# The last group's FFN in sixteen blocks of 256 tokens, with the layer norm of its first half among the blocks of the second

## The chip, the cores and the metric

The kernel runs on one NeuronCore of a Trainium2 chip. The time is the device time of one execution in microseconds (us). The kernel before takes 508.56 us (median of three runs, 507.5 to 508.71). Five engines work side by side and wait for one another through semaphores: PE (TensorE, the matmuls), DVE (VectorE), ACT (ScalarE), POOL (GpSimd) and SP (SyncE, which issues every DMA here).

## The reference

The input is 64 sequences of 64 tokens of 256 numbers, with a 64-number condition for each sequence. Layer 0 is a transformer block whose norms are scaled and shifted by the condition; layer 1 is a layer norm with a conditioned bias. What matters here is the end of it, cut to its core:

```
x   = x + a_alpha * attention(ada_rmsnorm(x))
y   = ada_rmsnorm(x)                                  # gamma, beta from the condition
ffn = silu(y @ gate_w.T) * (y @ hidden_w.T) @ out_w.T + out_b   # 256 -> 1024 -> 256
x   = x + f_alpha * ffn
out = (x - mean) * rsqrt(var + 1e-5) * weight + bias
out = (out + tanh(cond @ lin_w.T + lin_b)) * weight + bias
```

All is in float32. The matmuls with weights are made of three products of split operands: high part with high, low with high, high with low.

## The kernel before, in words

The 4096 tokens are cut into 8 groups (`g`) of 512 tokens, that is 8 sequences, or 4 tiles of 128 tokens. Each engine has its program written out by hand, in the order in which its instructions stand; nothing is reordered. The attention of group `g` is laid among the FFN blocks of group `g - 1`. `last(g)` is the program of each engine for the last group: first its attention among the FFN blocks of group 6 (there called `f`), and then the FFN of group 7 alone, with the layer norm of group 6 among its blocks, and at the end the layer norm of group 7 with nothing beside it. The change touches this last part only.

The 1024 hidden units are cut into 8 chunks of 128 (`CH = 8`). A block is one chunk for all 512 tokens and goes through the engines like this:

- PE, `gate_hidden` (L645): 12 matmuls with 512 columns, six into a gate bank and six into a hidden bank. The moving operand is `x2s`, in a high and a low part; ACT makes the high part (L893) and POOL the low (`x2_split`, L1379). For block 0 the program sorts the twelve, so that the four which need the low part come last.
- ACT, `tanh` (L867), reads the gate bank.
- DVE, `feed`: L1185 makes (tanh + 1) * gate, L1189 multiplies by half the hidden bank. Both leave their result in `act_t`.
- ACT, `hidden_hi` (L874): the rounded copy of `act_t`, the high part of `hs`.
- POOL, `hidden_lo` (L1413): the difference of the two, the low part of `hs`.
- PE, `ffn_out` (L662): 12 matmuls with 256 columns, which add the block to the output of 4 tiles in banks 0 and 1.

ACT takes `tanh(c)`, `hidden_hi(c)`, `tanh(c + 1)`, and so on, in this order, and `hidden_hi(c)` waits for DVE's second step of block c. In the last group `gate_hidden` alternates between two pairs of banks (2 and 3, 4 and 5), `act_t` and `hs` have two slots each, and `ffn_out(c - 2)` stands behind `gate_hidden(c)`: a lag of two blocks.

Behind the last `ffn_out`, DVE does `residual2` (L1201, L1204: times f_alpha, plus the residual `x2c`, on 4 tiles at once), the layer norm's sums (`sums_x3`, L1068, one instruction for each tile), means and variances (`stats_x3`, L1073 to L1077), the reciprocal root (`rsqrt`, L1022 to L1031: one estimate and three Newton rounds, ten small instructions, each of which waits for the one before), `mean_x3` (L1081), and then `finish_last` (L1212, L1217), two instructions for each of tiles 0 to 2. Tile 3 goes through ACT (`scale_x3`, L899) and POOL (L1497, L1499). SP stores the four tiles with a DMA for each (L412). For group 6 the same norm stands on DVE behind block 3 of group 7, on ACT (L899) behind block 4, and on POOL (L1403, L1409) behind block 4.

## Time and profile before

| | |
|---|---|
| median of 3 runs | 508.56 us (507.5 to 508.71) |
| the profiled execution's own time | 508.42 us |
| its span | 506.6 us |
| mean granted clock of PE | 0.987 of full speed |
| PE busy | 478.7 us, 94% of the span |
| DVE busy | 393.4 us, 78% |
| POOL busy | 271.4 us, 54% |
| ACT busy | 241.4 us, 48% |
| DMA | 44.21 MB, mean 87 GB/s |

The span is from the first to the last thing that the profiler saw; the execution's own time is 1.82 us longer. Starts are counted from the span's start. PE is busy throughout except for the last stretch. A share of busy time doesn't tell which engine decides: that is read from the waits at one place.

### The profile page before, as it was taken

The page shows a single profiled execution, that of the slowest core. Times are in us where ns is not written, and L with a number is a line of the kernel's source. Part 1 is how long each engine was busy: PE and PEld are TensorE (multiplying, and loading weights), DVE is VectorE, ACT ScalarE, POOL GpSimd, SP SyncE. Part 2 cuts the span into 40 slices and gives each one's busy share as a digit, 9 for nine tenths or more (in the row PEclk, how much of TensorE's full clock was granted, in tenths as well). Part 3 has the DMA queues.
Part 4 walks back from the last instruction along what each step waited for, and adds up shares of the span by engine and source line. Part 5 has one row for each costly group of instructions (what it writes and reads, how often), then busy time and mean ns, then how long its engine had stood idle before and what let it go on. Part 6 is the DMA issues. An engine that isn't in the chain of part 4 may idle for free.

```text
span 506.6 us, 11675 instructions
## 1 busy us (share of the span) xinstructions
PE 478.7 (94%) x4456; PEld 400.6 (79%) x4456; DVE 393.4 (78%) x776; ACT 241.4 (48%) x348; POOL 271.4 (54%) x179
## 2 busy tenths in 40 slices
PE   7888989999999999999999999999999999999990
PEld 4666878897878978888888978798788978888890
DVE  5868679778886888878895888878897789685636
ACT  3774743338352653438362563537354484414240
POOL 3447456454269445783269445684259543716471
PEclk9989999999999999999999999999999999999996
DMA  8463370206413082214503073023703062400131
GB/s 190 148 190 118 91 203 12 56 2 165 128 23 85 9 224 58 63 41 126 164 18 86 0 210 80 24 80 85 203 2 103 1 161 48 112 15 8 34 65 61
DMA packets 36058, 44.21 MB, mean 87 GB/s; under 512 B 3136, under 2 KB 31040, under 8 KB 36032
## 3 DMA queue, kind: packets, MB, share of 16 engines
q1 hardware_dynamic: 36032, 43.85, 32.5%
q8 instruction: 18, 0.29, 0.2%
q14 instruction: 8, 0.07, 0.1%
HBM read 35.18 MB, written 4.47 MB: 78 GB/s over the span
## 4 chain that ended last, share of the span: by engine, by line
PE 72%; DVE 7%; DMA 5%; ACT 4%; POOL 4%; issue 4%; SPq 2%; ACTq 0%; DVEq 0%; POOLq 0%
PE banks L645 26%; PE banks L662 16%; PE banks L465 7%; PE banks L563 5%; PE banks L497 4%; PE banks L595 4%; DMA row_b<-rows_dram 3%; PE banks L581 3%; PE banks L586 3%; DVE qpar L1113 1%; PE banks L423 1%; POOL hs L1413 1%; DMA xtok<-x_in 1%; DVE act_t L1185 1%; SPq L312 1%
## 5 line engine op out<-in xcount | busy, mean ns | idle before, releaser
L645 PE MATMUL banks<-x2s,gh 128*128 128x512 f32 x768 | 191.5, 398 | 5.1 <-DVE act_t L1185 4.6
L645 PEld LDWEIGHTS banks<-x2s,gh 128*128 128x128 f32 x768 | 139.9, 188 | 37.7 <-DVE act_t L1185 6.0
L1413 POOL TENSOR_TENSOR hs<-act_t,hs 128x512 fp32r<-128x512 f32 x64 | 83.0, 1301 | 96.0 <-ACT hs L874 96.0
L662 PE MATMUL banks<-wout,hs 128*128 128x256 f32 x768 | 105.1, 286 | 2.2 <-POOL hs L1413 2.1
L662 PEld LDWEIGHTS banks<-wout,hs 128*128 128x128 f32 x768 | 97.8, 188 | 8.1 <-POOL hs L1413 3.1
L874 ACT ACTIVATE hs<-act_t 128x512 fp32r<-128x512 f32 x64 | 40.3, 630 | 92.1 <-DVE act_t L1189 86.1
L867 ACT ACTIVATE act_t<-banks 128x512 f32<-128x512 f32 x64 | 38.2, 597 | 74.9 <-PE banks L645 71.9
L1185 DVE SCALAR_TENSOR_TENSOR act_t<-act_t,banks 128x512 f32<-128x512 f32 x64 | 43.9, 686 | 38.5 <-ACT act_t L867 37.3
L1136 DVE RECIPROCAL work_c<-banks 128x512 f32<-128x512 f32 x16 | 53.7, 3354 | 5.1 <-PE banks L581 5.1
L465 PE MATMUL banks<-xs,wqk 128*128 128x512 f32 x192 | 47.1, 393 | 2.3 <-POOL xs L1365 1.6
L1189 DVE SCALAR_TENSOR_TENSOR act_t<-act_t,banks 128x512 f32<-128x512 f32 x64 | 44.0, 687 | 5.9 <-PE banks L645 1.7
L465 PEld LDWEIGHTS banks<-xs,wqk 128*128 128x128 f32 x192 | 34.9, 188 | 10.1 <-POOL xs L1365 2.0
L1119 DVE TENSOR_REDUCE smax<-banks 128x16 bf16<-128x1024 f32 x32 | 37.6, 1217 | 2.7 <-PE banks L526 2.7
L1374 POOL TENSOR_TENSOR x2g<-x2g,tabs 128x512 f32<-128x512 f32 x16 | 16.4, 1043 | 42.6 <-DVE x2g L1178 42.6
L1389 POOL TENSOR_TENSOR x2c<-x,row_b 128x1024 f32<-128x1024 f32 x8 | 19.1, 2390 | 34.0 <-DMA row_b<-rows_dram 29.9
L563 PE MATMUL banks<-qpair,kpar 64*128 64x128 f32 x512 | 36.5, 282 | 0.8 <-issue 0.4
L563 PEld LDWEIGHTS banks<-qpair,kpar 64*128 64x128 f32 x512 | 31.2, 187 | 4.1 <-issue 2.7
L882 ACT ACTIVATE pt<-banks 128x1024 f32<-128x1024 f32 x32 | 31.9, 1018 | 4.2 <-PE banks L568 2.0
L822 ACT ACTIVATE kpair<-banks,cst 128x1024 bf16<-128x1024 f32 x16 | 17.0, 1110 | 22.4 <-PE banks L465 22.4
L1153 DVE TENSOR_TENSOR banks<-banks,row_aa 128x512 f32<-128x512 f32 x16 | 11.1, 694 | 19.4 <-PE banks L595 19.4
L1369 POOL TENSOR_TENSOR os<-work_c,os 128x512 fp32r<-128x512 f32 x16 | 20.6, 1289 | 8.1 <-ACT os L888 8.1
L497 PEld LDWEIGHTS banks<-wv,xs 128*128 128x128 f32 x192 | 24.1, 191 | 0.6
(118 smaller groups left out, 687.5 us busy)
## 6 DMA issues: line engine op xcount, KB each, us to landing
xtok<-x_in SPq DMA_DIRECT2D x8, 512.0 KB, 5.5
work_c<-xn SPq DMA_DIRECT2D x16, 256.0 KB, 3.5
xres<-x_in SPq DMA_DIRECT2D x8, 512.0 KB, 7.1
row_aa<-rows_dram SPq DMA_DIRECT2D x16, 256.0 KB, 6.7
row_af<-rows_dram SPq DMA_DIRECT2D x16, 256.0 KB, 5.9
row_b<-rows_dram SPq DMA_DIRECT2D x16, 256.0 KB, 6.4
shift<-rows_dram SPq DMA_DIRECT2D x16, 256.0 KB, 6.1
y<-final SPq DMA_DIRECT2D x7, 512.0 KB, 3.2
```

The lines of the kernel that those rows point to most:

```text
L465: last = mm(banks[:, base + m, :], wqk[:, a, k, c:c + P], xs[:, b, k, :], start=(n == 0), stop=(n == 5))
L497: last = mm(banks[:, base + t // 2, D * (t % 2):D * (t % 2) + D], xs[:, a, k, P * t:P * t + P], wv[:, b, k, :], start=(n == 0), stop=(n == 5))
L563: mm(region(i, half), kpar[r, h, b], qpair[r, h, :, L * b:L * b + L], start=(i == 0), stop=False)
L645: last = mm(banks[:, base + part, :], gh[:, a, k, w:w + P], x2s[:, b, k, :], start=(n == 0), stop=(n == 5))
L662: last = mm(banks[:, t // 2, D * (t % 2):D * (t % 2) + D], hs[:, c % 2, b, P * t:P * t + P], wout[:, a, c, :], start=(c == 0 and a == b an ...
L867: nc.scalar.activation(act_t[:, c % 2, :], banks[:, base, :], ACT.Tanh, scale=0.5)\
L874: nc.scalar.activation(hs[:, c % 2, 0, :], act_t[:, c % 2, :], ACT.Copy).then_inc(h_hi, 1)
L1119: V.tensor_reduce(smax[:, :, 8 * n:8 * n + 8], banks[:, base:base + 2, :].rearrange("p a (x c) -> p a x c", c=L), AX.X, ALU.max).then_inc( ...
L1136: V.reciprocal(work_c[:, 0, :], banks[:, den_bank, :]).then_inc(o_steps, 1)
L1185: V.scalar_tensor_tensor(out=a, in0=a, scalar=1.0, in1=banks[:, base, :], op0=ALU.add, op1=ALU.mult).then_inc(h_steps, 1)
L1189: V.scalar_tensor_tensor(out=a, in0=a, scalar=0.5, in1=banks[:, base + 1, :], op0=ALU.mult, op1=ALU.mult).then_inc(h_steps, 1)
L1413: tt(hs[:, c % 2, 1, :], act_t[:, c % 2, :], hs[:, c % 2, 0, :].bitcast(F32), ALU.subtract)\
```

## The change

The FFN of group 7 is done in two halves of 256 tokens, eight blocks for tiles 0 and 1 and then eight for tiles 2 and 3, so 16 half blocks `n`. A half block has 12 matmuls of 256 columns in `gate_hidden_half`, 6 in `ffn_out_half`, and instructions of half the width on ACT, DVE and POOL. There are three pairs of banks (6 and 7, 2 and 3, 4 and 5) instead of two and four half slots of `act_t` and `hs` instead of two whole ones, and `ffn_out_half(n - 3)` stands behind `gate_hidden_half(n)`. The first half's output lies in bank 0, the second's in bank 1. The order of the matmuls of block 0 is no longer sorted.

The norm of group 6 is spread on DVE behind half blocks 3, 4 and 5, on ACT behind 6 and 7, and on POOL behind 7 to 10, in halves. `residual2` of the first half of group 7 stands on DVE behind half block 11, its sums and variances behind 12, its reciprocal root behind 13; ACT scales tiles 0 and 1 (two instructions) between half blocks 14 and 15; POOL weights and shifts them behind its last `hidden_lo_half`. Behind the last half block, DVE does tiles 2 and 3 alone. There are three stores at the end: tiles 0 and 1 together, tile 2, tile 3. In the diff, lines inside `build` stand eight columns further left than in the file.

```diff
 WARM_LOADS, WARM_MAX, WARM_OUTPUT, WARM_NORM = 3, 4, 16, 4
-LAST_DVE = 3
+HALF = TOK // 2
+BLOCKS = 2 * CH
...
     return not isinstance(g, int) or g > 1
+def half_slot(a, n):
+    s = n % 4
+    return a[:, s // 2, ..., HALF * (s % 2):HALF * (s % 2) + HALF]
+def half_base(n):
+    return (6, 2, 4)[n % 3]
+def x3_half(h):
+    return banks[:, h, :].rearrange("p (t n) -> p t n", t=2)
...
     def load_shift(f):
         if later(f):
-            sp.wait_ge(final_steps, FS * f)
+            sp.wait_ge(final_steps, FS * f + (FS if is_last(f) else 0))
         load_rows(shift, R_SHIFT, f, ld_shift)
...
     load_af(GROUPS - 1)
-    store(GROUPS - 2)
+    sp.wait_ge(final_steps, FS * (GROUPS - 2) + 2 * FS)
+    sp.dma_start(out_v[GROUPS - 2], final[:, :, :]).then_inc(out_stored, 16)
     load_shift(GROUPS - 1)
-    for t in range(TT):
-        if t < LAST_DVE:
-            sp.wait_ge(last_dve, LAST_DVE + t + 1)
-        else:
-            sp.wait_ge(last_pool, 2 * (t - LAST_DVE) + 2)
+    sp.wait_ge(last_pool, 2)
+    sp.dma_start(out_v[GROUPS - 1][:, 0:2], final[:, 0:2, :]).then_inc(out_stored, 16)
+    for t in range(2, TT):
+        sp.wait_ge(last_dve, t + 1)
         sp.dma_start(out_v[GROUPS - 1][:, t], final[:, t, :]).then_inc(out_stored, 16)
-    sp.wait_ge(out_stored, 16 * (GROUPS - 1 + TT))
+    sp.wait_ge(out_stored, 16 * (GROUPS - 1 + 3))
...
+    def gate_hidden_half(g, n):
+        base, half, c = half_base(n), n // CH, n % CH
+        tokens = slice(HALF * half, HALF * half + HALF)
+        if n == 0:
+            pe.wait_ge(x2s_hi, KD * g + KD)
+        for part in range(2):
+            if n >= LAG:
+                pe.wait_ge(h_steps, 2 * CH * g + 2 * (n - LAG) + part + 1)
+            elif n > 0 and part == 0:
+                pe.wait_ge(h_steps, 2 * CH * g - 2 * (2 - n))
+            for i, (k, a, b) in enumerate(passes):
+                if n == 0 and part == 0 and b:
+                    pe.wait_ge(x2s_lo, KD * g + k + 1)
+                w = HID * part + P * c
+                last = mm(banks[:, base + part, 0:HALF], gh[:, a, k, w:w + P], x2s[:, b, k, tokens],
+                          start=(i == 0), stop=(i == 5))
+            last.then_inc((gate_mm, hidden_mm)[part], 1)
+    def ffn_out_half(g, n):
+        half, c = n // CH, n % CH
+        h = half_slot(hs, n)
+        if n == 0:
+            pe.wait_ge(x3_steps, X3 * g)
+        pe.wait_ge(h_hi, CH * g + n + 1)
+        for a, b in ((0, 0), (1, 0), (0, 1)):
+            if b:
+                pe.wait_ge(h_lo, CH * g + n + 1)
+            for t in range(2):
+                last = mm(banks[:, half, D * t:D * t + D], h[:, b, P * t:P * t + P], wout[:, a, c, :],
+                          start=(c == 0 and a == b and t == 0), stop=(c == CH - 1 and b == 1 and t == 1))
         last.then_inc(out_mm, 1)
...
-        gate_hidden(g, 0, alternate=True)
+        gate_hidden_half(g, 0)
         ffn_out(f, 7)
-        gate_hidden(g, 1, alternate=True)
-        for c in range(2, CH):
-            gate_hidden(g, c, alternate=True)
-            ffn_out(g, c - 2)
-        for c in range(CH - 2, CH):
-            ffn_out(g, c)
+        for n in range(1, LAG):
+            gate_hidden_half(g, n)
+        for n in range(LAG, BLOCKS):
+            gate_hidden_half(g, n)
+            ffn_out_half(g, n - LAG)
+        for n in range(BLOCKS - LAG, BLOCKS):
+            ffn_out_half(g, n)
...
+    def feed_half(g, n):
+        a = half_slot(act_t, n)
+        free = CH * g + n - 3 if n >= 4 else CH * g - 1 + n // 2
+        act.wait_ge(gate_mm, CH * g + n + 1)
+        act.wait_ge(h_lo, free)
+        nc.scalar.activation(a, banks[:, half_base(n), 0:HALF], ACT.Tanh, scale=0.5).then_inc(tanh_ready, 1)
+        act.wait_ge(h_steps, 2 * CH * g + 2 * n + 2)
+        act.wait_ge(out_mm, free)
+        nc.scalar.activation(half_slot(hs, n)[:, 0, :], a, ACT.Copy).then_inc(h_hi, 1)
...
-        for c in range(CH):
-            feed(g, c, 2 + 2 * (c % 2))
-            if c == 4:
-                scale_x3(g - 1)
-        scale_x3(g, range(LAST_DVE, TT), banks[:, 0:2, :].rearrange("p a (t n) -> p (a t) n", t=2))
+        for n in range(BLOCKS):
+            feed_half(g, n)
+            if n == 6:
+                scale_x3(g - 1, range(0, 2))
+            if n == 7:
+                scale_x3(g - 1, range(2, TT))
+            if n == BLOCKS - 2:
+                act.wait_ge(out_stored, 16 * g)
+                scale_x3(g, range(0, 2), x3_half(0))
...
+    def feed_half(g, n):
+        a = half_slot(act_t, n)
+        base = half_base(n)
+        dve.wait_ge(tanh_ready, CH * g + n + 1)
+        V.scalar_tensor_tensor(out=a, in0=a, scalar=1.0, in1=banks[:, base, 0:HALF], op0=ALU.add,
+                               op1=ALU.mult).then_inc(h_steps, 1)
+        dve.wait_ge(h_steps, 2 * CH * g + 2 * n + 1)
+        dve.wait_ge(hidden_mm, CH * g + n + 1)
+        V.scalar_tensor_tensor(out=a, in0=a, scalar=0.5, in1=banks[:, base + 1, 0:HALF], op0=ALU.mult,
+                               op1=ALU.mult).then_inc(h_steps, 1)
+    def alpha_half(g, h):
+        dve.wait_ge(ld_af, 32 * g + 32)
+        dve.wait_ge(out_mm, CH * g + CH * h + CH)
+        y = x3_half(h)
+        V.tensor_tensor(y, y, row_af[:, 2 * h:2 * h + 2, :], ALU.mult).then_inc(x3_steps, 1)
+    def add_half(g, h):
+        dve.wait_ge(x3_steps, X3 * g + 2 * h + 1)
+        dve.wait_ge(x2_kept, g + h + 1)
+        y = x3_half(h)
+        V.tensor_tensor(y, y, x2c[:, 2 * h:2 * h + 2, :], ALU.add).then_inc(x3_steps, 1)
+    def sums_half(g, h):
+        dve.wait_ge(x3_steps, X3 * g + 2 * h + 2)
+        for t in range(2):
+            V.bn_stats(stat[:, 2 * h + t, :], x3_half(h)[:, t, :]).then_inc(ln_stats, 1)
+    def stats_half(g, h):
+        tiles = slice(2 * h, 2 * h + 2)
+        done = LS * g + 5 * h
+        dve.wait_ge(ln_stats, done + 2)
+        V.memset(nt1[:, 2, 1, tiles], 0.0)
+        for t in range(2 * h, 2 * h + 2):
+            V.bn_aggr(mv[:, t, :], stat[:, t, :]).then_inc(ln_stats, 1)
+        dve.wait_ge(ln_stats, done + 4)
+        V.tensor_scalar(nt1[:, 0, 1, tiles], mv[:, tiles, 1], EPS_LN, None, ALU.add).then_inc(ln_stats, 1)
+    def rsqrt_half(g, h):
+        tiles = slice(2 * h, 2 * h + 2)
+        dve.wait_ge(ln_stats, LS * g + 5 * h + 5)
+        dve.wait_ge(ln_scaled, TT * g)
+        v, y, t = (nt1[:, i, 1, tiles] for i in range(3))
+        rsqrt(norm1_steps, RS * (g + 3 + h), v, y, t)
+    def finish_half(g):
+        x3 = x3_half(1)
+        for t in range(2):
+            V.scalar_tensor_tensor(out=x3[:, t, :], in0=x3[:, t, :], scalar=mv[:, 2 + t, 0:1],
...
+        dve.wait_ge(ld_shift, 32 * g + 32)
+        dve.wait_ge(out_stored, 16 * g)
+        for t in range(2):
+            dve.wait_ge(last_dve, t + 1)
+            V.scalar_tensor_tensor(out=final[:, 2 + t, :], in0=x3[:, t, :],
+                                   scalar=nt1[:, 1, 1, 2 + t:3 + t], in1=shift[:, 2 + t, :], op0=ALU.mult,
+                                   op1=ALU.add).then_inc(last_dve, 1)
...
-        feed(g, 0)
+        feed_half(g, 0)
         residual2(f)
-        for c in range(1, CH):
-            feed(g, c, 2 + 2 * (c % 2))
-            if c == 3:
-                layer_norm(f, g + 2)
-        residual2(g, in_place=True)
-        layer_norm(g, g + 3, x3_banks())
-        finish_last(g, range(LAST_DVE))
+        for n in range(1, BLOCKS):
+            feed_half(g, n)
+            if n == 3:
+                dve.wait_ge(x3_steps, X3 * g)
+                sums_x3(final)
+            if n == 4:
+                stats_x3(f)
+            if n == 5:
+                dve.wait_ge(ln_stats, LS * g)
+                rsqrt_both(g + 2)
+                mean_x3()
+            if n == 11:
+                alpha_half(g, 0)
+                add_half(g, 0)
+            if n == 12:
+                sums_half(g, 0)
+                stats_half(g, 0)
+            if n == 13:
+                rsqrt_half(g, 0)
+                dve.wait_ge(norm1_steps, RS * (g + 4))
+                V.scalar_tensor_tensor(out=mean_rs[:, 0:2], in0=mv[:, 0:2, 0], scalar=-1.0,
+                                       in1=nt1[:, 1, 1, 0:2], op0=ALU.mult, op1=ALU.mult).then_inc(ln_mean, 1)
+        alpha_half(g, 1)
+        add_half(g, 1)
+        sums_half(g, 1)
+        stats_half(g, 1)
+        rsqrt_half(g, 1)
+        finish_half(g)
...
+    w2_half = w2[:, :].unsqueeze(1).to_broadcast([P, 2, D])
+    def hidden_lo_half(g, n):
+        pool.wait_ge(h_hi, CH * g + n + 1)
+        h = half_slot(hs, n)
+        tt(h[:, 1, :], half_slot(act_t, n), h[:, 0, :].bitcast(F32), ALU.subtract).then_inc(h_lo, 1)
+    def keep_half(g, h):
+        tiles = slice(2 * h, 2 * h + 2)
+        pool.wait_ge(x3_steps, X3 * g)
+        pool.wait_ge(ld_b, 32 * g + 32)
+        pool.wait_ge(x2_steps, X2 * g + X2)
+        tt(x2c[:, tiles, :], x2[:, tiles, :], row_b[:, tiles, :], ALU.add).then_inc(x2_kept, 1)
+    def weight_half(f, h):
+        tiles = slice(2 * h, 2 * h + 2)
+        pool.wait_ge(ln_scaled, TT * f + 2 * h + 2)
+        tt(final[:, tiles, :], final[:, tiles, :], w2_half, ALU.mult).then_inc(final_steps, 1)
+    def shift_half(f, h):
+        tiles = slice(2 * h, 2 * h + 2)
+        pool.wait_ge(final_steps, FS * f + 2 * h + 1)
+        pool.wait_ge(ld_shift, 32 * f + 32)
+        tt(final[:, tiles, :], final[:, tiles, :], shift[:, tiles, :], ALU.add).then_inc(final_steps, 1)
...
-        for c in range(CH):
-            hidden_lo(g, c)
-            if c == 1:
-                keep_x2(g)
-            if c == 4:
-                weight_x3(f)
-                shift_x3(f)
+        for n in range(BLOCKS):
+            hidden_lo_half(g, n)
+            if n in (2, 3):
+                keep_half(g, n - 2)
+            if n in (7, 9):
+                weight_half(f, (n - 7) // 2)
+            if n in (8, 10):
+                shift_half(f, (n - 8) // 2)
+        pool.wait_ge(ln_scaled, TT * g + 2)
+        tt(final[:, 0:2, :], final[:, 0:2, :], w2_half, ALU.mult).then_inc(last_pool, 1)
+        pool.wait_ge(last_pool, 1)
         pool.wait_ge(ld_shift, 32 * g + 32)
-        for n, t in enumerate(range(LAST_DVE, TT)):
-            pool.wait_ge(ln_scaled, TT * g + n + 1)
-            tt(final[:, t, :], final[:, t, :], w2[:, :], ALU.mult).then_inc(last_pool, 1)
-            pool.wait_ge(last_pool, 2 * n + 1)
-            tt(final[:, t, :], final[:, t, :], shift[:, t, :], ALU.add).then_inc(last_pool, 1)
+        tt(final[:, 0:2, :], final[:, 0:2, :], shift[:, 0:2, :], ALU.add).then_inc(last_pool, 1)
```

In the rows of the program below, a line begins with its number in the kernel that it is of; x2 behind it means that the instruction stands there twice.

PE, from the end of group 6's FFN: L645, L660 and L697 are gate and hidden matmuls, L662, L677 and L712 those of the output. Before:

```order
L662 MATMUL banks<-wout,hs 128x256 x24
L645 MATMUL banks<-x2s,gh 128x512 x12
L662 MATMUL banks<-wout,hs 128x256 x12
L645 MATMUL banks<-x2s,gh 128x512 x24
L662 MATMUL banks<-wout,hs 128x256 x12
```

and now:

```order
L677 MATMUL banks<-wout,hs 128x256 x24
L697 MATMUL banks<-x2s,gh 128x256 x12
L677 MATMUL banks<-wout,hs 128x256 x12
L697 MATMUL banks<-x2s,gh 128x256 x36
L712 MATMUL banks<-wout,hs 128x256 x6
L697 MATMUL banks<-x2s,gh 128x256 x12
L712 MATMUL banks<-wout,hs 128x256 x6
```

Group 6's last output block stands behind one block of group 7, as before, but that block is half as long; then three half blocks go ahead before the first output of group 7. The pair of the last two rows goes on to the end, where the last three outputs stand together.

DVE, behind half block 11 of group 7 and up to half block 13 (L1276 and L1280 are the two steps of a half block, L1287 and L1293 `alpha_half` and `add_half`, L1087 the first instruction of `rsqrt`). Before, at the end of the last group's blocks:

```order
L1185 SCALAR_TENSOR_TENSOR act_t<-act_t,banks 128x512
L1189 SCALAR_TENSOR_TENSOR act_t<-act_t,banks 128x512
L1201 TENSOR_TENSOR banks<-banks,row_af 128x1024
L1204 TENSOR_TENSOR banks<-banks,x2c 128x1024
L1068 BN_STATS stat<-banks 128x6 x4
L1073 MEMSET nt 128x4
L1075 BN_AGGR mv<-stat 128x2 x4
L1077 TENSOR_SCALAR nt<-mv 128x4
L1022 TENSOR_SCALAR nt<-nt 128x8
```

and now:

```order
L1287 TENSOR_TENSOR banks<-banks,row_af 128x512
L1293 TENSOR_TENSOR banks<-banks,x2c 128x512
L1276 SCALAR_TENSOR_TENSOR act_t<-act_t,banks 128x256
L1280 SCALAR_TENSOR_TENSOR act_t<-act_t,banks 128x256
L1298 BN_STATS stat<-banks 128x6 x2
L1305 MEMSET nt 128x2
L1307 BN_AGGR mv<-stat 128x2 x2
L1309 TENSOR_SCALAR nt<-mv 128x2
L1276 SCALAR_TENSOR_TENSOR act_t<-act_t,banks 128x256
L1280 SCALAR_TENSOR_TENSOR act_t<-act_t,banks 128x256
L1087 TENSOR_SCALAR nt<-nt 128x2
```

The norm of tiles 0 and 1 has moved from behind the last block into the gaps behind half blocks 11, 12 and 13; that of tiles 2 and 3 is still behind the last.

ACT, at its end (L867 and L959 tanh, L874 and L962 the high part, L899 and L949 the norm's scaling). Before:

```order
L867 ACTIVATE act_t<-banks 128x512
L874 ACTIVATE hs<-act_t 128x512
L867 ACTIVATE act_t<-banks 128x512
L874 ACTIVATE hs<-act_t 128x512
L899 ACTIVATE final<-banks,mean_rs,nt 128x256
```

and now:

```order
L959 ACTIVATE act_t<-banks 128x256
L962 ACTIVATE hs<-act_t 128x256
L949 ACTIVATE final<-banks,mean_rs,nt 128x256 x2
L959 ACTIVATE act_t<-banks 128x256
L962 ACTIVATE hs<-act_t 128x256
```

The scaling stood behind the last block, for one tile; now it stands ahead of the last half block's tanh, for two.

## Rows read from the trace of the kernel before

**Rows 1.** The stretch of the last group's FFN alone, busy time by engine

```profile
459.20:494.50 35.30, 35.30 (x206) 30.89 (x204) 17.74 (x39) 11.47 (x20) 20.44 (x14) 1.00 0.19 41
```

**Rows 2.** The timeline, PE: start, duration, what, count, idle time before

```profile
458.59 0.76 PE L662 MATMUL banks<-wout,hs 128*128 128x256 f32 x4 [0.29 <-POOL hs L1413]
459.18 2.95 PE L645 MATMUL banks<-x2s,gh 128*128 128x512 f32 x12
461.97 1.59 PE L662 MATMUL banks<-wout,hs 128*128 128x256 f32 x12
463.40 5.74 PE L645 MATMUL banks<-x2s,gh 128*128 128x512 f32 x24
490.04 4.46 PE L662 MATMUL banks<-wout,hs 128*128 128x256 f32 x36
```

**Rows 3.** The timeline, DVE, behind the last matmul

```profile
494.63 1.23 DVE L1201 TENSOR_TENSOR banks<-banks,row_af 128x1024 f32<-128x1024 f32 x1 [3.22 <-PE banks L662]
495.90 1.23 DVE L1204 TENSOR_TENSOR banks<-banks,x2c 128x1024 f32<-128x1024 f32 x1
497.17 1.42 DVE L1068 BATCH_NORM_STATS2 stat<-banks 128x6 f32<-128x256 f32 x4
498.64 0.17 DVE L1075 BATCH_NORM_AGGREGATE mv<-stat 128x2 f32<-128x6 f32 x1
...
499.25 0.17 DVE L1022 TENSOR_SCALAR nt<-nt 128x8 int32<-128x8 int32 x1
...
501.33 1.27 DVE L1212 SCALAR_TENSOR_TENSOR banks<-banks,mv,w 128x256 f32<-128x256 f32 x3
502.51 1.26 DVE L1217 SCALAR_TENSOR_TENSOR final<-banks,nt,shift 128x256 f32<-128x256 f32 x3
```

**Rows 4.** The last stores: the timeline of SP, and the issues (KB, us to landing)

```profile
503.01 1.81 SPq L412 DMA_DIRECT2D y<-final  x4
y<-final SPq DMA_DIRECT2D x4, 128.0 KB, 1.8
```

**Rows 5.** The timeline, ACT and DVE, around blocks 5 and 6

```profile
481.00 2.07 ACT L899 ACTIVATE final<-final,mean_rs,nt 128x256 f32<-128x256 f32 x4
482.98 0.57 ACT L867 ACTIVATE act_t<-banks 128x512 f32<-128x512 f32 x1
...
483.58 0.69 DVE L1185 SCALAR_TENSOR_TENSOR act_t<-act_t,banks 128x512 f32<-128x512 f32 x1 [3.15 <-ACT act_t L867]
...
484.31 0.69 DVE L1189 SCALAR_TENSOR_TENSOR act_t<-act_t,banks 128x512 f32<-128x512 f32 x1
...
485.03 0.63 ACT L874 ACTIVATE hs<-act_t 128x512 fp32r<-128x512 f32 x1 [1.47 <-DVE act_t L1189]
485.56 0.58 ACT L867 ACTIVATE act_t<-banks 128x512 f32<-128x512 f32 x1
```

**Rows 6.** Groups by line and shape: count, busy us, mean ns

```profile
L867 ACT ACTIVATE act_t<-banks 128x512 f32<-128x512 f32 x64 | 38.2, 597 | 74.9 <-PE banks L645 71.9 <-POOL hs L1413 2.6
L923 ACT ACTIVATE shift<-shift 64x256 f32<-64x256 f32 x1 | 0.4, 418 | 0.0
L899 ACT ACTIVATE final<-banks,mean_rs,nt 128x256 f32<-128x256 f32 x1 | 0.6, 563 | 9.1 <-DVE mean_rs L1081 9.1
L1037 DVE COPY tabs<-banks 128x256 f32<-128x256 f32 x2 | 0.8, 420 | 0.1
L1212 DVE SCALAR_TENSOR_TENSOR banks<-banks,mv,w 128x256 f32<-128x256 f32 x3 | 1.3, 482 | 0.0
L1497 POOL TENSOR_TENSOR final<-final,w 128x256 f32<-128x256 f32 x1 | 0.7, 722 | 8.4 <-ACT final L899 8.4
```

**Rows 7.** The timeline, DVE, at the end of group 6's FFN

```profile
463.70 1.23 DVE L1201 TENSOR_TENSOR banks<-banks,row_af 128x1024 f32<-128x1024 f32 x1
...
466.11 0.68 DVE L1185 SCALAR_TENSOR_TENSOR act_t<-act_t,banks 128x512 f32<-128x512 f32 x1
```

**Rows 8.** The timeline, POOL: the low parts, at two places

```profile
457.25 1.29 POOL L1413 TENSOR_TENSOR hs<-act_t,hs 128x512 fp32r<-128x512 f32 x1
458.50 2.52 POOL L1379 TENSOR_TENSOR x2s<-x2g,x2s 128x512 fp32r<-128x512 f32 x2
460.99 1.29 POOL L1413 TENSOR_TENSOR hs<-act_t,hs 128x512 fp32r<-128x512 f32 x1
```

**Rows 9.** The timeline, DVE and POOL, at one moment of the loop

```profile
373.65 1.92 POOL L1351 TENSOR_TENSOR xn<-xn,tabs 128x1024 f32<-128x1024 f32 x1
...
373.76 1.82 DVE L1026 TENSOR_TENSOR nt<-nt 128x8 f32<-128x8 f32 x1
...
375.62 0.17 DVE L1028 SCALAR_TENSOR_TENSOR nt<-nt 128x8 f32<-128x8 f32 x1
```

More of the change, by code:

```diff
@@ L56 @@
 WARM_LOADS, WARM_MAX, WARM_OUTPUT, WARM_NORM = 3, 4, 16, 4
-LAST_DVE = 3
+HALF = TOK // 2
+BLOCKS = 2 * CH
+LAG = 3
 ZEROED = 1
@@ L665, in ffn_out @@
                 last.then_inc(out_mm, 1)
+            def gate_hidden_half(g, n):
[27 more added lines that the diff above has]
+                                  start=(c == 0 and a == b and t == 0), stop=(c == CH - 1 and b == 1 and t == 1))
+                last.then_inc(out_mm, 1)
             def head(g, ln=True):
@@ L1193, in x3_banks, with residual2 @@
                 return banks[:, 0:2, :].rearrange("p a (t n) -> p (a t) n", t=2)
-            def residual2(f, in_place=False):
+            def residual2(f):
                 dve.wait_ge(ld_af, 32 * f + 32)
@@ L1203, in residual2 @@
                 dve.wait_ge(x2_kept, f + 1)
[L1204 to L1218 removed]
+                V.tensor_tensor(final[:, :, :], y, x2c[:, :, :], ALU.add).then_inc(x3_steps, 1)
@@ L1276, in main, with layer_norm @@
                 norm2(g)
-            def layer_norm(f, n, x3=final):
+            def layer_norm(f, n):
                 dve.wait_ge(x3_steps, X3 * (f + 1))
-                sums_x3(x3)
+                sums_x3(final)
                 stats_x3(f)
```

13 lines of the change are left out of this document (1 added, 12 removed).

## Prediction

> **What bounds the kernel now.** I read first the busy time by stretch, then PE's timeline, then DVE's and SP's behind the last matmul, and last ACT's and DVE's inside one block. The change touches only what comes after 459 us, so only this is weighed.
>
> From 459.2 to 494.5 us PE is busy in 35.30 of 35.30 us, at the full granted clock (1.00, that is 2.4 GHz), while DVE is busy 17.74, POOL 20.44 and ACT 11.47 us [rows 1]. PE alone sets this stretch. Its last matmul ends at 490.04 + 4.46 = 494.50 us [rows 2]. I call that moment T. Behind it stands a tail of 506.6 - 494.5 = 12.1 us in which PE has nothing to do: DVE from 494.63 to 502.51 + 1.26 = 503.77 us [rows 3], then the last of four stores, which are issued at 503.01 + 1.81 = 504.82 us at the latest, that is 0.45 us each, and land 1.8 us later [rows 4].
>
> So there are two questions. How much shorter is the tail for two tiles than for four? And where does T come to lie: is the stretch ahead of it still PE's?
>
> **The tail gets shorter by 3.3 us.** Step by step, from rows 3:
> - L1201 takes a step of 495.90 - 494.63 = 1.27 us for 1024 elements. For 512 elements DVE takes 0.69 us [rows 5], so a step of 0.73. The same for L1204. Saved: 0.54 + 0.55 = 1.09.
> - Four sums take 498.64 - 497.17 = 1.47 us, 0.33 us for each but the last. Two: 0.80. Saved 0.67.
> - Four means and variances, from 498.64 to the estimate at 499.25, 0.61 us; two fewer of about 0.08 save 0.15.
> - The root and `mean_x3` take 501.33 - 499.25 = 2.08 us, eleven instructions whose time doesn't depend on width. The ten of the root stay; `mean_x3` goes, 0.08.
> - L1212: 502.51 - 501.33 = 1.18 us for three, 0.39 each, so 0.79 for two. L1217 the same. Saved 0.39 + 0.40.
> - The stores. Before, the fourth issue began at 504.82 - 0.45 = 504.37 us, 0.60 us behind the last data, since four issues of 0.45 us queue up. Now tile 3 is ready 0.39 us behind tile 2, and its issue can begin 0.45 us behind tile 2's: about 0.09 us behind its own data. Saved 0.5.
>
> Sum: 3.3 us. The tail is 12.1 - 3.3 = 8.8 us. The first half's work on POOL (two instructions of about 1.25 us behind the last low part) and its store end before DVE's, so they cost nothing.
>
> **PE's own work gets longer by 2 us.** Matmuls of 256 columns follow each other at (463.40 - 461.97) / 12 = 0.119 us, those of 512 at (5.74 - 0.16) / 24 = 0.233 us [rows 2]. A half block of gate and hidden is 12 x 0.119 = 1.43 us where half of a whole one was 1.40; with the output's 0.715 the period is 2.145 us.
>
> Block 0 isn't sorted any more. PE starts it at 459.18 us as before. Four matmuls take it to 459.66; the fifth and sixth need the low parts of `x2s`, which POOL finishes at 459.77 and 458.50 + 2.52 = 461.02 us [rows 8]. The sixth goes at about 461.2, and the hidden half behind it ends its issue at 462.0, where the whole block 0 had ended at 461.97. The wait of 1.1 us is about what the shorter block saves. Group 6's last output block follows, and its end is at 463.62 us, against 463.56 before [rows 2]: no loss here.
>
> From there on PE alone would need 15 x 1.43 + 16 x 0.715 = 32.9 us, which would put T at 463.45 + 32.9 + 0.17 (a matmul's end behind its step) = 496.5 us. This is a floor.
>
> **But the half blocks form a chain through ACT and DVE, and it is this chain that I expect to set T.** Look at ACT and DVE in a whole block [rows 5]: tanh starts at 482.98, DVE's first step at 483.58, its second at 484.31, the high part at 485.03 and the next tanh at 485.56. These are 0.60 + 0.73 + 0.72 + 0.53 = 2.58 us from one tanh to the next, and none of the four can begin earlier, because ACT takes the next tanh only behind this block's high part. It was harmless with a period of 2.79 + 1.43 = 4.22 us. How much of it is fixed? DVE does 1024 elements in 1.23 us and 512 in 0.69, so 256 save 0.27 more: 0.42, and L1037 shows that size at 0.420 [rows 3, 5, 6]. ACT's tanh is 597 ns at 512 and 418 at 256 (64 partitions) [rows 6], about 0.20 less. So a half block takes c = 2.58 - 2 x 0.27 - 2 x 0.205 = 1.63 us against a period of 2.145: halving the work takes only 37% off the chain. Only 0.5 us of slack for each half block is left, and everything that the change inserts between two half blocks on DVE or ACT must fit in it.
>
> The Trainium skill, page "VectorE: DVE Perf Modes", section on the fixed extra latency of SBUF-source operations, says the same in general: latency is exposed between instructions, so that many small tiles pay it each time, and tiles should have 512 elements or more. By its table (224 + N cycles at 1.2 GHz) an estimate for the high part of a half block is 0.40 us; rows 5 and 6 make it 0.42, and the sum goes by these.
>
> After DVE's second step of half block n starts (I call this X), DVE is free at X + 0.34 and wanted again at X + 0.45 + 0.325 + 0.405 = X + 1.18. An insert of length i on DVE delays the chain by 0.34 + i - 1.18, if that is positive. An insert on ACT counts in full.
>
> The chain starts with group 6's `residual2`, which stands on DVE between half blocks 0 and 1: matmul end 463.62 + 0.12 (494.63 - 494.50) [rows 3], then 466.11 - 463.70 = 2.41 us [rows 7] makes 466.15; X(1) = 466.60. Then:
> - 14 half blocks of 1.63: 22.82 us.
> - Behind 3, four sums, 1.36: 0.52 us. Behind 4, variances, 0.6 us: none.
> - Behind 5, root and mean, 2.15 us (2.08 and a gap): 1.31 us.
> - Behind 6 and 7 on ACT, four scalings at (482.98 - 481.00) / 4 = 0.495 us [rows 5]: 1.98.
> - Behind 11, `alpha_half` and `add_half`, 0.73 + 0.63: 0.52.
> - Behind 12, sums and variances, 1.25: 0.41; with POOL in the way (below) 0.57.
> - Behind 13, root and mean: 1.31. Behind 14 on ACT, two scalings: 0.99.
>
> One more thing is in the way. A DVE instruction on the small `nt` tiles which normally takes 0.17 us took 1.82 us at 373.76, until 375.58, exactly to the end of a POOL instruction that had begun just before it (373.65 + 1.92 = 375.57) [rows 9]. POOL's low part of half block n begins at X + 0.45 + 0.43 + 0.08 = X + 0.96 and takes 0.72 us (L1497) [rows 6], so it always falls into a root that runs from X + 0.34 to X + 2.49. I count 0.6 us for each of the two roots: 1.2. The Trainium skill, page "SBUF — State Buffer", section "Who interferes with whom", states that a DVE instruction with two SBUF inputs, or in a two-port mode, waits for the whole of a GpSimd instruction that reads SBUF. The trace agrees, 1.82 us against 0.17 in rows 9. By that rule the feed steps, with one input in PSUM, never wait; without it the sum would be 1.4 us lower.
>
> Sum of the delays: 0.52 + 1.31 + 1.98 + 0.52 + 0.57 + 1.31 + 0.99 + 1.2 = 8.4 us. X(15) = 466.60 + 22.82 + 8.4 = 497.8 us. Then the high part (0.45 + 0.51), the low part 0.73, PE's start behind POOL 0.04 and its last two matmuls 0.52 (four took 0.76 after such a wait [rows 2]) make T = 500.1 us, 3.6 us above PE's floor and 5.6 later than before.
>
> On the way PE's banks are also watched: `gate_hidden_half(11)` can start at 483.5 and needs half block 8 through DVE, which by the same steps is at 482.8. It is the tightest place; no stall, 0.7 us to spare.
>
> **Sum.** T is 5.6 us later, the tail 3.3 us shorter: 2.3 us longer. The profiled execution took 508.42 us, so 510.7. Its time is 0.14 us under the median of the runs, which is less than I can work out; I say 510.7 us.
>
> **Bounds.** The shapes that rows don't show are the 128x256 feed steps. Below, c can't be under what DVE and ACT show without any gap, 0.42 x 4 - 0.1 of overlap = 1.55: T 1.1 us earlier. Above, the nearest rows of the same shape, L1212 at 482 and L899 at 563 ns [rows 6], would add 2 x 0.06 + 2 x 0.14 = 0.4 us to c, 6 us in all; but both have per-partition operands that the feed steps lack, so I take 0.42. Each POOL collision is between 0 and 0.7 us.
>
> **Rivals.**
> 1. PE stays the bound: the chain keeps up, as three blocks of lag and three bank pairs allow. For it: PE is 100% busy before [rows 1], and DVE is busy for half of the time, ACT for a third. Against it: the lag lets PE run ahead, but doesn't shorten the time from the last gate matmul to the last output, nor ACT's strict order. T would be 496.5, the span 496.5 + 8.8 = 505.3, the time 507.1 us: not slower. It decides if the delays of 8.4 us are under 4.8.
> 2. A lighter chain: c is 1.57 rather than 1.63 (0.8 us over 14) and the roots meet no POOL instruction (1.2 us). Time 508.7 us, no difference. For it: from 499.25 us on the trace has a root without any such wait [rows 3]; against it, the moment of the low part is tied to the root's by the order of the program.
> 3. A heavier chain: DVE's half steps take 0.48 us like L1212, 15 x 0.12 = 1.8 us more, so 512.5 us, and then the margin of 0.7 us at half block 11 is gone too, and PE stalls in the middle.
>
> **Chances.** What a measurement of this kernel can tell from no change is about 0.3%, 1.5 us: under 507.0 is faster, over 510.1 slower. My forecast 0.52 (its own range 509.4 to 512.2, a sixth of it under 510.1); rival 1 0.13; rival 2 0.18; rival 3 0.17. Slower: five sixths of the forecast, 0.43, and rival 3, 0.17: 0.60. Faster: two thirds of rival 1, whose 507.1 us lies at the edge and would come with anything missed in the tail: 0.09. Same: the other third, 0.04, rival 2, and the rest of the forecast, 0.09: 0.31. The range is 507.9 to 512.9: it leaves out most of rival 1 and the far end of rival 3.
>
> **What the profile after would show.** Matmuls L697 at 0.119 us each and a wait of about 1.1 us in block 0 on L1513 (POOL). Tanh to tanh 1.63 us where nothing is inserted. Between half blocks 13 and 15 the longest gaps on ACT and PE: PE's last outputs waiting on POOL's `hs`, with the chain that ended last going through ACT and DVE instead of PE from about 466 us on. T near 500 and a tail of 8.8 us. The forecast is wrong if PE has no idle time between 485 and 498 us (then rival 1), or if tanh to tanh is 1.75 us or more (rival 3), or if the tail isn't shorter by about 3 us.

## The result, and the profile after

The changed kernel takes 509.86 us (median of seven runs, 509.29 to 510.50) against 508.56 us before; the ratio is 1.0026, with a 95% interval of 1.0015 to 1.0036. It is slower, by little. The prediction was 510.7 us, with 507.9 to 512.9 as its range. By the classes that the prediction set itself (slower from 510.1 us on) the measured median counts as no change, to which it gave 0.31, and not as slower, to which it gave 0.60. The profiled execution spans 508.3 us where 508.9 was worked out (506.6 + 2.3) and 506.6 was the span before.

The first view is PE's timeline behind 458 us (start, duration, line, count, idle before and what ended it); it answers to [rows 2]:

```profile
458.64 0.73 PE L677 MATMUL banks<-wout,hs 128*128 128x256 f32 x4 [0.31 <-POOL hs L1547]
459.21 1.06 PE L697 MATMUL banks<-x2s,gh 128*128 128x256 f32 x5
461.10 1.10 PE L697 MATMUL banks<-x2s,gh 128*128 128x256 f32 x7 [0.84 <-POOL x2s L1513]
462.04 1.58 PE L677 MATMUL banks<-wout,hs 128*128 128x256 f32 x12
463.46 4.44 PE L697 MATMUL banks<-x2s,gh 128*128 128x256 f32 x36
...
493.42 1.58 PE L712 MATMUL banks<-wout,hs 128*128 128x256 f32 x12
495.44 1.31 PE L712 MATMUL banks<-wout,hs 128*128 128x256 f32 x6 [0.44 <-ACT hs L962]
497.99 1.61 PE L712 MATMUL banks<-wout,hs 128*128 128x256 f32 x6 [1.23 <-ACT hs L962]
```

PE waits in block 0 (0.84 us, where about 1.1 was expected), then works without a gap to 495 us, and then waits twice for the high part from ACT (0.44 and 1.23 us). The prediction had named POOL's low part for these gaps; PE waits for that only 0.06 us, ahead of its last two matmuls, but it is what they start behind. The last matmul ends at 497.99 + 1.61 = 499.60 us instead of 494.50. PE has no gap in the middle: what is late at the end was late all the way, hidden by the lag.

DVE's timeline shows where the time is. Here are half blocks 2 and 3, with nothing inserted, and then 13 to 15:

```profile
467.79 0.42 DVE L1276 SCALAR_TENSOR_TENSOR act_t<-act_t,banks 128x256 f32<-128x256 f32 x1 [0.76 <-ACT act_t L959]
468.24 0.42 DVE L1280 SCALAR_TENSOR_TENSOR act_t<-act_t,banks 128x256 f32<-128x256 f32 x1
469.42 0.42 DVE L1276 SCALAR_TENSOR_TENSOR act_t<-act_t,banks 128x256 f32<-128x256 f32 x1 [0.76 <-ACT act_t L959]
...
490.76 0.41 DVE L1276 SCALAR_TENSOR_TENSOR act_t<-act_t,banks 128x256 f32<-128x256 f32 x1
...
492.33 0.59 DVE L1091 TENSOR_TENSOR nt<-nt 128x2 f32<-128x2 f32 x1
...
494.07 0.41 DVE L1276 SCALAR_TENSOR_TENSOR act_t<-act_t,banks 128x256 f32<-128x256 f32 x1
...
496.61 0.42 DVE L1276 SCALAR_TENSOR_TENSOR act_t<-act_t,banks 128x256 f32<-128x256 f32 x1 [1.67 <-ACT act_t L959]
497.06 0.42 DVE L1280 SCALAR_TENSOR_TENSOR act_t<-act_t,banks 128x256 f32<-128x256 f32 x1
499.70 0.70 DVE L1287 TENSOR_TENSOR banks<-banks,row_af 128x512 f32<-128x512 f32 x1 [2.22 <-PE banks L712]
```

From one first step to the next it is 469.42 - 467.79 = 1.63 us, to the hundredth what was worked out from whole blocks [rows 5, 6]. With the root between, it is 494.07 - 490.76 = 3.31 us, so the root (with the mean behind it) costs 1.68; with ACT's two scalings between, 496.61 - 494.07 = 2.54, so they cost 0.91. And the chain that ended last goes, over this stretch, by turns through DVE and ACT (start, duration, what):

```profile
467.39 0.38 ACT act_t L959
467.79 0.43 DVE act_t L1276
468.24 0.43 DVE act_t L1280
468.70 0.02 ACT hs L962
468.72 0.07 issue
468.81 0.21 issue
469.02 0.38 ACT act_t L959
```

Before, the same stretch of that chain was PE alone, for instance:

```profile
469.14 1.43 PE banks L662 x12
470.57 2.78 PE banks L645 x12
```

That DVE and ACT look idle in the changed kernel (12.79 and 8.18 us busy of the 20 us from 465 on) is therefore no sign that they don't decide.

### The profile page after: what moved, and what is told of

It reads as the page before. It is cut to its first block, busy times and chain, and to the rows that moved or that the text cites. A ratio compares the mean times of both kernels' runs of the same rounds, so it can differ in the third digit from the quotient of the medians.

```text
span 508.3 us, 11953 instructions
## 1 busy us (share of the span) xinstructions
PE 480.9 (95%) x4552; PEld 406.0 (80%) x4552; DVE 396.9 (78%) x804; ACT 243.8 (48%) x365; POOL 274.5 (54%) x190
## 4 chain that ended last, share of the span: by engine, by line
PE 69%; DVE 11%; ACT 5%; issue 5%; POOL 4%; DMA 3%; SPq 1%; ACTq 0%; DVEq 0%; POOLq 0%
PE banks L660 23%; PE banks L677 15%; PE banks L480 8%; PE banks L578 6%; PE banks L512 4%; PE banks L610 4%; PE banks L596 3%; PE banks L601 3%; DMA row_b<-rows_dram 2%; DVE qpar L1178 1%; PE banks L583 1%; DVE act_t L1250 1%; PE banks L631 1%; DVE act_t L1276 1%; POOL hs L1547 1%
## 5 line engine op out<-in xcount | busy, mean ns | idle before, releaser
L660 PE MATMUL banks<-x2s,gh 128*128 128x512 f32 x672 | 168.3, 399 | 5.1 <-DVE act_t L1250 4.7
L660 PEld LDWEIGHTS banks<-x2s,gh 128*128 128x128 f32 x672 | 122.2, 188 | 34.3 <-DVE act_t L1250 6.1
L1547 POOL TENSOR_TENSOR hs<-act_t,hs 128x512 fp32r<-128x512 f32 x56 | 72.8, 1303 | 83.1 <-ACT hs L924 83.0
L677 PE MATMUL banks<-wout,hs 128*128 128x256 f32 x672 | 92.6, 286 | 1.4 <-POOL hs L1547 1.3
L677 PEld LDWEIGHTS banks<-wout,hs 128*128 128x128 f32 x672 | 85.5, 188 | 6.6 <-POOL hs L1547 2.0
L924 ACT ACTIVATE hs<-act_t 128x512 fp32r<-128x512 f32 x56 | 35.3, 630 | 76.1 <-DVE act_t L1254 76.1
L917 ACT ACTIVATE act_t<-banks 128x512 f32<-128x512 f32 x56 | 33.5, 599 | 67.6 <-PE banks L660 65.8
L1250 DVE SCALAR_TENSOR_TENSOR act_t<-act_t,banks 128x512 f32<-128x512 f32 x56 | 38.5, 687 | 23.2 <-ACT act_t L917 22.0
L1254 DVE SCALAR_TENSOR_TENSOR act_t<-act_t,banks 128x512 f32<-128x512 f32 x56 | 38.5, 688 | 5.5 <-PE banks L660 2.0
L1523 POOL TENSOR_TENSOR x2c<-x,row_b 128x1024 f32<-128x1024 f32 x7 | 16.7, 2389 | 32.3 <-DMA row_b<-rows_dram 29.0
L697 PE MATMUL banks<-x2s,gh 128*128 128x256 f32 x192 | 25.7, 283 | 0.9 <-POOL x2s L1513 0.8
```

The lines of the kernel that those rows point to most:

```text
L660: last = mm(banks[:, base + part, :], gh[:, a, k, w:w + P], x2s[:, b, k, :], start=(n == 0), stop=(n == 5))
L677: last = mm(banks[:, t // 2, D * (t % 2):D * (t % 2) + D], hs[:, c % 2, b, P * t:P * t + P], wout[:, a, c, :], start=(c == 0 and a == b an ...
L917: nc.scalar.activation(act_t[:, c % 2, :], banks[:, base, :], ACT.Tanh, scale=0.5)\
L924: nc.scalar.activation(hs[:, c % 2, 0, :], act_t[:, c % 2, :], ACT.Copy).then_inc(h_hi, 1)
L1250: V.scalar_tensor_tensor(out=a, in0=a, scalar=1.0, in1=banks[:, base, :], op0=ALU.add, op1=ALU.mult).then_inc(h_steps, 1)
L1254: V.scalar_tensor_tensor(out=a, in0=a, scalar=0.5, in1=banks[:, base + 1, :], op0=ALU.mult, op1=ALU.mult).then_inc(h_steps, 1)
```

## The experiments

Up to the changed part the profiles already differ by up to 2.1 us, so positions are counted from one point that all have: the start of the four matmuls of group 6's last-but-one output that wait for POOL (458.59 us before, 458.64 in the changed kernel, 457.09 in e4, 459.22 in e7). T is the end of the last matmul, and "end" the end of the span.

| kernel | T | end | median us | against before |
|---|---|---|---|---|
| before | 35.91 | 48.01 | 508.56 | |
| the changed one | 40.96 | 49.66 | 509.86 | 1.0026 [1.0015, 1.0036] |
| e1_tanh_ahead | 37.93 | 46.62 | 507.28 | 0.9972 [0.9945, 0.9999] |
| e2_root_behind | 38.11 | 48.29 | 508.28 | 1.0004 [0.9987, 1.0021] |
| e3_scale_behind | 39.76 | 48.48 | 508.86 | 1.0008 [0.9991, 1.0024] |
| e6_norm_behind | 37.79 | 49.91 | 509.79 | 1.0046 [1.0025, 1.0066] |
| e7_ahead_sorted | 37.48 | 46.18 | 506.23 | 0.9959 [0.9941, 0.9976] |
| e9_lag_two | 40.80 | 49.49 | 508.91 | 1.0028 [1.0010, 1.0045] |
| e10_ahead_lag_two | 38.74 | 47.47 | 507.27 | 0.9983 [0.9965, 1.0001] |
| e5_low_memset | 39.83 | 48.59 | 508.30, one run | |
| e4_sorted | 40.26 | 49.01 | 508.05, one run | |
| e11_pe_warm | 40.68 | 49.38 | 509.93, one run | |

Each ratio is against runs of the kernel before on the same chip, so medians of different rows are not to be subtracted. The positions are from one profile each. "One run" means that a kernel was timed once.

**e1_tanh_ahead: cut the chain.** Only the order on ACT is changed, nothing is taken away:

```diff
-                for n in range(BLOCKS):
-                    feed_half(g, n)
+                tanh_half(g, 0)
+                for n in range(BLOCKS):
+                    if n + 1 < BLOCKS:
+                        tanh_half(g, n + 1)
+                    hi_half(g, n)
```

> ACT takes the tanh of half block n + 1 ahead of the high part of half block n; nothing else is changed. My theory (the time of the changed kernel is set by the chain tanh, DVE, DVE, high part, next tanh, 1.63 us for each half block, with every insert on top): the chain is cut, inserts on DVE and ACT overlap with PE again, PE becomes the bound. Last matmul at 496.5 to 497.0 us instead of 499.6, no idle time of PE over 0.3 us behind block 0, span about 505.4, time about 507.0 against 509.9 of the changed kernel and 508.6 of the one before. Rival A (the cost lies on PE: more matmuls, the wait in block 0): no change, 509.9. Rival B (the cost is the norm's instructions on DVE and ACT themselves, whatever the order): at most 0.5 us, 509.4.

The last matmul comes 3.0 us earlier, and the kernel is just faster than the one before: the interval of the ratio ends at 0.9999. ACT and PE at the end of it:

```profile
488.36 0.38 ACT L959 ACTIVATE act_t<-banks 128x256 f32<-128x256 f32 x1 [1.45 <-PE banks L697]
488.64 0.41 ACT L965 ACTIVATE hs<-act_t 128x256 fp32r<-128x256 f32 x1
490.50 0.38 ACT L959 ACTIVATE act_t<-banks 128x256 f32<-128x256 f32 x1 [1.45 <-PE banks L697]
```

```profile
491.74 1.59 PE L697 MATMUL banks<-x2s,gh 128*128 128x256 f32 x12
493.17 3.14 PE L712 MATMUL banks<-wout,hs 128*128 128x256 f32 x24
```

ACT now waits for PE, a tanh every 490.50 - 488.36 = 2.14 us, which is PE's period, and PE has no idle time behind block 0. With the same matmuls and the same norm in the same places, rivals A (PE's own cost) and B (the norm's own time) fall: the 3.0 us were the strict order.

**e2_root_behind and e3_scale_behind: take inserts off the chain.**

```diff
-                    if n == 13:
+                    if n == BLOCKS - 1:
                         rsqrt_half(g, 0)
...
-                    if n == BLOCKS - 2:
+                    if n == BLOCKS - 1:
                         act.wait_ge(out_stored, 16 * g)
```

e3 has the second hunk alone, e2 both.

> The reciprocal root of the first half moves on DVE from behind half block 13 to behind half block 15, and with it ACT's two scalings from behind 14 to behind 15. ACT's order stays strict. My theory: each insert counts in the chain with what the trace after shows (root 1.68 us, scalings 0.91), so DVE's last second step starts at 494.5 instead of 497.06 and the last matmul ends at about 496.9; the root then lies in DVE's idle time before that and ends at about 497.3, so the tail begins 2.3 us earlier than now: span 506.0, time 507.5. Rival A (PE): the last matmul doesn't move, and the root behind the last block comes on top: 510 or more. Rival B (norm's instructions themselves): no change, 509.9.

> Only ACT's two scalings of the first half move from behind half block 14 to behind 15. My theory: the last tanh comes 0.9 us earlier, and so does the last matmul: 498.7, time 508.9 to 509.0. If PE or DVE set the end, nothing changes: 509.9.

e3 moved T by 1.2 us, 0.9 by the scalings and the rest by the last matmuls (see e11 below). e2 moved it by 2.85, of which 1.68 + 0.91 are the inserts. The places are right, but e2's time isn't: 507.5 was expected, and 508.28 was measured. The second half's tail begins, behind the root, where I put it, 38.76 us from the common point (38.7 by the forecast), yet from there to the end it is 9.5 us, where the changed kernel takes 508.3 - 499.70 = 8.6. The reason is in DVE's and POOL's timelines of e2:

```profile
499.12 1.12 DVE L1087 TENSOR_SCALAR nt<-nt 128x2 int32<-128x2 int32 x1
500.28 0.16 DVE L1091 TENSOR_TENSOR nt<-nt 128x2 f32<-128x2 f32 x1
```

```profile
497.62 1.26 POOL L1657 TENSOR_TENSOR final<-final,w 128x512 f32<-128x512 f32 x1 [2.46 <-ACT final L949]
498.96 1.26 POOL L1660 TENSOR_TENSOR final<-final,shift 128x512 f32<-128x512 f32 x1
```

POOL's work on the first half, late by as much as the root, now runs into the second half's root: one instruction waits from 499.12 to 500.24, where POOL ends at 500.22. A step that hides well itself can uncover its successor on another engine.

**e6_norm_behind: the halves without the norm among them.** The calls of `alpha_half` to `rsqrt_half` of half 0 stand behind the loop, and the scalings behind half block 15.

> The whole norm of the first half (alpha, add, sums, variances, root) moves on DVE from behind half blocks 11, 12 and 13 to behind 15, and ACT's scalings to behind 15: the halves alone, without the norm among the blocks. My theory: delays of 0.5, 0.43, 1.68 and 0.91 us leave the chain, which then reaches PE's floor: last matmul at 496.5. DVE has 4.8 to 5.2 us of norm to do from 494.1, so the second half's tail begins at about 499.2, 2.7 us behind the last matmul: span 507.8, time 509.4, half a microsecond less than with the norm among the blocks. If the norm among the blocks is worth its place (its 5 us hidden behind PE), this is slower than the changed kernel by 2 us or more: 512.

T falls to PE's floor, 37.79 us (37.9 by the sum), and DVE starts the second half's tail 2.6 us behind it (at 497.95, with T at 495.38 us in this profile). Against the changed kernel the end is 0.25 us later where 0.5 us earlier was expected; the same collision with POOL is in it (1.12 us for one instruction). So, with ACT's strict order, the norm among the blocks gained next to nothing over leaving it at the end: it hid 5 us of DVE behind PE and gave them back through the chain. The run shows one thing more. ACT's order is still strict here, and T is as early as in e1. The order alone costs nothing at the end; it costs because it makes what stands between two half blocks count.

**e9_lag_two and e10_ahead_lag_two: the third block of lag.** The edit is `LAG = 2`, in e10 on top of e1.

> The changed kernel with a lag of two half blocks instead of three: gate_hidden_half(n) waits for half block n - 2, and ffn_out_half(n - 2) stands behind it. ACT's order stays strict. My theory: the end is set by the chain through ACT and DVE, so the lag is worth nothing there: PE waits in the middle (half block 11 could start at 483.4 and needs half block 9, at 484.2), but the last matmul stays 37.6 us behind the start of group 6's last output block, and the time 509.9 us within 0.3. Rival (the third pair of banks and the third block of lag hide what the halves cost): later by the stalls in the middle, 1 us or more, 511.

> The tanh ahead of the high part, as in e1_tanh_ahead, with a lag of two. My theory: with the chain cut, a half block's results are ready about 2.1 us behind its start on DVE, and the inserts are what a lag has to cover: the root behind half blocks 5 and 13 (2.1 to 2.5 us) delays the next half block's DVE steps by about that, which two blocks of 2.14 us still hide. The same as e1 within 0.3 us: 507.3. If the third block of lag is needed, PE shows waits on DVE's L1276 or L1280 lines behind the roots, 0.5 us or more each.

With the strict order the lag is worth nothing: T 40.80 against 40.96 us, and the 0.16 us are in the last six matmuls (1.41 instead of 1.61 us). The stall of 0.8 us that I had expected in the middle didn't come, though. With a lag of two, one more output stands ahead of `gate_hidden_half(11)`, which I had not counted, and PE loses only 0.12 us ahead of half block 3 and 0.04 ahead of 10.

With the order cut the third block of lag is worth 0.8 us (38.74 against 37.93), and not where I looked for it. There are no waits on DVE behind the roots in the middle. PE's last gate and hidden block starts 0.81 us later (492.40 - 458.23 = 34.17 against 491.74 - 458.38 = 33.36), 0.71 for the output that now stands ahead of it and 0.1 for a wait ahead of half block 3, and with it the last half block's way through ACT, DVE and POOL. The times don't tell the two apart: 0.9972 and 0.9983 have overlapping intervals.

**e5_low_memset: POOL out of the root's way.**

```diff
+                if n in (5, 13):
+                    nc.gpsimd.memset(h[:, 1, :].bitcast(F32), 0.0).then_inc(h_lo, 1)
+                    return
```

> The changed kernel, but POOL fills the low part of half blocks 5 and 13 with zeros instead of computing it (so those low parts are left out of the result): an instruction that only writes. My theory: the wait of 0.42 us inside each of the two roots (one of the ten instructions takes 0.59 us instead of 0.17) comes from POOL's reading instruction, and goes; nothing else in the chain changes, so the last matmul comes 0.8 us earlier relative to group 6's last output block: 36.7 us instead of 37.6, time about 509.0. Rival (the longer instruction has nothing to do with what POOL does): both roots keep their 0.59 us.

In the changed kernel, a step of the root behind half block 13 and POOL's instruction beside it:

```profile
492.33 0.59 DVE L1091 TENSOR_TENSOR nt<-nt 128x2 f32<-128x2 f32 x1
492.15 0.74 POOL L1555 TENSOR_TENSOR hs<-act_t,hs 128x256 fp32r<-128x256 f32 x1 [1.33 <-ACT hs L962]
```

DVE and POOL at half block 13 of e5:

```profile
490.99 0.16 DVE L1096 SCALAR_TENSOR_TENSOR nt<-nt 128x2 f32<-128x2 f32 x1
491.19 0.16 DVE L1091 TENSOR_TENSOR nt<-nt 128x2 f32<-128x2 f32 x1
491.38 0.16 DVE L1093 SCALAR_TENSOR_TENSOR nt<-nt 128x2 f32<-128x2 f32 x1
```

```profile
491.00 0.31 POOL L1556 MEMSET hs<- 128x256 f32 x1 [1.31 <-ACT hs L962]
```

Both 0.59 us instructions are 0.17 us long here, so the wait came from POOL's instruction. Whether it came from its reading, as I had it, or from its length, these lines can't tell. The held steps end 0.02 to 0.03 us behind POOL's end. The memset is over at 491.31, and L1091 ends at 491.35 by its own length, so a step that waited for the memset would have looked the same. One step bears on it, at half block 5. It starts 0.01 us behind the memset and isn't held, while in e7 a step that starts 0.01 us behind POOL's low part is held for its whole length. First e5, then e7:

```profile
473.83 0.17 DVE L1096 SCALAR_TENSOR_TENSOR nt<-nt 128x8 f32<-128x8 f32 x1
473.82 0.31 POOL L1556 MEMSET hs<- 128x256 f32 x1 [0.71 <-ACT hs L962]
```

```profile
474.55 0.75 DVE L1101 TENSOR_TENSOR nt<-nt 128x8 f32<-128x8 f32 x1
474.54 0.73 POOL L1565 TENSOR_TENSOR hs<-act_t,hs 128x256 fp32r<-128x256 f32 x1 [1.41 <-ACT hs L969]
```

That is one case, at the profile's resolution: it speaks for the reading and doesn't show it. T is 1.13 us earlier: 0.84 of it are the two waits, and the last six matmuls take 1.31 instead of 1.61 us.

**e4_sorted and e11_pe_warm: the two small terms.** e4 sorts half block 0 as before the change; e11 puts matmuls whose result nothing reads into PE's last two waits:

```diff
+                    if n == BLOCKS - 2:
+                        pe.wait_ge(h_steps, 2 * CH * g + 2 * 14)
+                        warm_up(wqk[:, 0, 0], 4, 2)
+                    if n == BLOCKS - 1:
+                        warm_up(wqk[:, 0, 0], 8, 2)
```

> The changed kernel with half block 0 sorted again (the four matmuls which need x2s's low parts come last), and ACT's order strict as in the change. My theory: the chain starts with group 6's residual, which waits for group 6's last output block; that block comes 0.45 us earlier, and so does everything behind it. From group 6's last-but-one output (the four matmuls behind the wait on POOL's hs) to the last matmul: 40.5 us instead of 40.96, and to the end of the span 49.2 instead of 49.7. Rival (PE's wait in block 0 is hidden in a kernel whose end is set by ACT and DVE): no change.

> The changed kernel, with four matmuls of 512 columns ahead of the output of half block 14 and eight ahead of that of 15, into a bank that nothing reads, so that PE works while it waits (0.9 us and 1.9 us). The trace after shows a mean granted clock of 0.70 between 497.9 and 499.6 us, behind a wait of 1.23 us, and the last two matmuls take 0.80 us. My theory: these 0.3 us are the half clock, and with PE at work they take about 0.5 us at a granted clock of 1.00; if the twelve end before the low part of half block 15 arrives, the last matmul comes 0.3 us earlier relative to the same point (40.65 us instead of 40.96); if they run into it, up to as much later. Rival (the last two matmuls are long for another reason, such as loading weights after a wait): still 0.8 us.

e4 moved T by 0.70 us: 0.44 because group 6's last output starts 2.95 us behind the common point instead of 3.40, and 0.26 because the last six matmuls took 1.35 us instead of 1.61. So the wait of PE in block 0 did reach the end, through group 6's residual at the head of the chain. In e11 the last six take 0.87 us and don't wait for the low part any more, which is there before they start. The windows show the clock (start:end, length, PE busy, granted clock, DMA share, GB/s), first of the changed kernel, the last six and then the last two alone, then of e11:

```profile
497.90:499.60 1.70, 1.55 (x6) 0.70 0.00 0
498.75:499.60 0.85, 0.80 (x2) 0.50 0.00 0
```

```profile
497.90:499.60 1.70, 1.49 (x10) 1.00 0.00 0
```

The clock of the changed kernel fell to the lower level (1.2 GHz) during the last six, after waits of 0.44 and 1.23 us, and the last two, which start behind the low part, ran at it in full: 0.80 us. With PE at work it stayed at the higher, and T came 0.28 us earlier. That the clock makes the last two long, and not the wait ahead of them, is shown by e5. There the same wait of 1.23 us stands ahead of the last six, and the clock stayed up through the last two:

```profile
497.20:497.74 0.54, 0.50 (x2) 1.00 0.00 0
```

**e7_ahead_sorted: the version that the experiments point to**, e1 and e4 together.

> The tanh ahead of the high part, as in e1_tanh_ahead, and the matmuls of half block 0 sorted again, so that the four which need the low parts of x2s come last. My theory: with the chain cut, PE is the bound, and what is taken off its wait in block 0 comes off the end. That wait is 0.84 us now; sorted, eight matmuls of 0.119 us stand ahead of the four, which then wait for the same POOL instruction, so group 6's last output block starts about 0.45 us earlier and the last matmul ends about 34.1 us behind the point where that block started before, against 34.5 in e1: time 0.4 to 0.5 us under e1's, 506.8, and 1.5 us under the kernel before. Rival (the order of block 0 doesn't matter, since group 6's last low part comes from POOL at the same time): no gain over e1.

506.23 us, 0.9959 of the kernel before (0.9941 to 0.9976): the lowest of all, and clearly under the kernel before. T is 0.45 us earlier than in e1, as forecast; the times alone don't tell the two apart, since the intervals of their ratios overlap.

## Why the prediction was right

- The tail: 508.3 - 499.6 = 8.7 us, forecast 8.8. The steps on DVE came as worked out (0.74 us from 499.70 to the next, the root at 0.2 a step), and so did the stores.
- The chain: right in its mechanism and its base, 1.63 us. Its sum was 0.7 us too high: X(15) at 497.06 instead of 497.8 us. The term that was mis-sized is above all POOL's collision. Each root cost 1.68 us (1.67 behind half block 5) where 1.31 + 0.6 were counted; 0.42 of it is the collision, since the step that runs when POOL starts isn't held, only the next one (at 492.33, POOL having started at 492.15). Behind half block 12 the delay was 0.44, not 0.57. The rest are differences under 0.1 us in the other inserts.
- The end of the chain was undersized by 0.3 us: 2.54 instead of 2.26 us from X(15) to T. I took four matmuls behind a short wait (0.29 us, [rows 2]) as the measure for the last two, and their clock had fallen: 0.80 us at 0.50 of full speed instead of 0.50 us at full speed in e5.
- PE's side: the period of 2.14 us is as forecast, and so are the start of group 6's last output (462.04 us, 462.0 forecast) and the clear passage at half block 11. The wait in block 0 was 0.84 us instead of about 1.1. I said that the wait costs nothing "against 463.56 before". That is true, and yet e4 shows that it cost: sorted, the same short block would have been 0.45 us ahead.
- Rival 1 (PE stays the bound) is what e1 makes of the kernel: T at 37.93 us from the common point, that is 496.6 in the changed kernel's time, where its floor was 496.5. Rival 2's chain without collisions is e5's, but its lighter half block (1.57 us) didn't come: it takes 1.63 us. Rival 3 falls: DVE's half steps take 0.42 us.
- The lower bound of the range's working has a slip: 0.42 x 4 - 0.1 is 1.58 us and not 1.55, so T could be 0.7 us earlier by it and not 1.1. Nothing hangs on it, since 1.63 came.

In sum: 0.7 us too much for the chain, 0.3 too little behind it, 0.1 too much for the tail, which leaves 510.2 us: errors of both signs, which in part cancelled. The profiled execution took 510.44 us (2.14 us outside its span instead of 1.82), and the median of the runs is 509.86: the remaining difference is what executions differ by.
